# Gated cross-attention block, 16 x 256 tokens over 1601 keys: maxima split on VectorE and moved within SBUF, keys in four blocks, a beginning of its own for step 0, a new order of TensorE's work

## The reference

```python
def attention(v, k, q, ...):            # v = k = ctx, q = layernorm(x)
    qh, kh, vh = (split_heads(a @ w.T + b) for ...)
    logits = einsum('bhqd,bhkd->bhqk', qh, kh) / sqrt(8)
    out = einsum('bhqk,bhkd->bhqd', softmax(logits), vh)
    return out.reshape(B, S, 128) @ dense_w.T + dense_b

x = x + tanh(g_xattn[0]) * attention(ctx, ctx, layernorm(x))
# feed-forward: sigmoid gate of 8 experts, the two best, weights normalised, plus one shared expert
h = gelu(einsum('bsd,edh->bseh', xn, W1) + b1)
y = einsum('bseh,ehd->bsed', h, W2) + b2
x = x + tanh(g_ffn[0]) * (einsum('bse,bsed->bsd', gate_full, y) + gelu(xn @ Ws1 + bs1) @ Ws2 + bs2)
```

## Time and profile before

| | |
|---|---|
| median of 3 runs | 1435.47 us (1433.91 to 1437.52) |
| the profiled execution's own time | 1436.73 us |
| its span | 1434.9 us |
| TensorE matmul busy | 1241.7 us, 87% |
| VectorE busy | 1049.3 us, 73% |
| ScalarE busy | 1055.6 us, 74% |
| GpSimd busy | 418.7 us, 29% |
| granted TensorE clock, mean | 0.902 |

### The profile page before, as it was taken

The page is one execution under the profiler, slowest core; times in us unless marked ns, Lnnn a source line. Parts: engine busy times, 40 slices in busy tenths (PEclk is TensorE's granted clock), DMA queues, the critical chain, the costliest instruction groups (busy, mean ns, idle before and its releaser), DMA issues.

```text
span 1434.9 us, 29778 instructions
## 1 busy us (share of the span) xinstructions
PE 1241.7 (87%) x11555; PEld 458.9 (32%) x11555; DVE 1049.3 (73%) x1208; ACT 1055.6 (74%) x1962; POOL 418.7 (29%) x309
## 2 busy tenths in 40 slices
PE   2448889798989999899989999799979999799855
PEld 1112323232323433243323333243323433243224
DVE  8477778587768888688868878688768868689001
ACT  1008879587978799688968789688968889689741
POOL 7242224051333215151424125051423205010111
PEclk6568999798988999899989999899989999899786
DMA  7673634636273653737273744637173744501101
GB/s 213 114 149 69 150 70 98 140 84 129 53 164 70 139 119 87 147 81 149 52 169 61 170 87 99 139 82 146 47 167 67 165 92 96 102 11 33 31 14 45
DMA packets 71390, 147.13 MB, mean 103 GB/s; under 512 B 13705, under 2 KB 37970, under 8 KB 71250
## 3 DMA queue, kind: packets, MB, share of 16 engines
q1 hardware_dynamic: 71250, 145.24, 47.4%
HBM read 88.30 MB, written 56.91 MB: 101 GB/s over the span
## 4 chain that ended last, share of the span: by engine, by line
PE 66%; DMA 14%; ACT 5%; DVE 4%; SPq 4%; POOL 3%; issue 2%; POOLq 0%; ACTq 0%; DVEq 0%
PE o_ps L775 26%; PE a_ps L757 15%; PE b_ps L741 11%; DMA m_dram<-nm_parts 10%; PE a_ps L688 4%; PE a_ps L692 4%; ACT probs L573 3%; PE b_ps L720 2%; DVE run_max L901 2%; SPq L406 2%; DMA q_op<-m_dram 1%; SPq L397 1%; PE a_ps L684 1%; PE b_ps L723 1%; DMA q_op<-q_dram 1%
## 5 line engine op out<-in xcount | busy, mean ns | idle before, releaser
L901 DVE TENSOR_REDUCE run_max<-b_ps 128x2 f32<-128x1024 f32 x768 | 899.4, 1218 | 249.4 <-PE b_ps L741 246.0
L573 ACT ACTIVATE probs<-a_ps 128x512 f32<-128x512 f32 (+1 forms) x1664 | 901.9, 594 | 144.3 <-PE a_ps L757 127.4
L775 PE MATMUL o_ps<-probs,v_op 128*32 128x256 f32 (+3 forms) x4928 | 505.8, 483 | 2.3 <-ACT probs L573 1.2
L757 PE MATMUL a_ps<-q_op,k_op 51*128 51x256 bf16 (+1 forms) x3328 | 338.1, 283 | 46.4 <-DMA q_op<-m_dram 25.6
L741 PE MATMUL b_ps<-k_op,q_op 48*128 48x512 bf16 (+1 forms) x2048 | 325.6, 350 | 37.5 <-DVE run_max L901 24.2
L757 PEld LDWEIGHTS a_ps<-q_op,k_op 51*128 51x128 bf16 (+1 forms) x3328 | 112.9, 97 | 373.5 <-ACT probs L573 307.3
L741 PEld LDWEIGHTS b_ps<-k_op,q_op 48*128 48x128 bf16 x2048 | 88.7, 96 | 208.2 <-DVE run_max L901 95.9
L775 PEld LDWEIGHTS o_ps<-probs,v_op 128*32 128x32 f32 (+1 forms) x4928 | 98.4, 109 | 176.4 <-issue 93.8
L509 POOL TENSOR_TENSOR attn<-num,den_all 128x256 f32<-128x256 f32 x16 | 11.6, 728 | 440.3 <-DMA den_all<-r_dram 440.3
L688 PE MATMUL a_ps<-kctx,wk_s 128*128 128x400 f32 (+1 forms) x128 | 81.4, 734 | 55.7 <-DMA kctx<-ctx_t 49.9
L469 POOL TENSOR_TENSOR nm_parts<-nm_t,one 8x256 bf16<-8x256 f32 x32 | 19.3, 602 | 360.5 <-ACT nm_t L605 360.5
(11 more groups left out here) (100 smaller groups left out, 680.4 us busy)
## 6 DMA issues: line engine op xcount, KB each, us to landing
k_op<-k_dram SPq DMA_DIRECT2D x64, 600.4 KB, 9.5
k_dram<-k_parts SPq DMA_DIRECT2D x32, 600.4 KB, 6.0
kctx<-ctx_t SPq DMA_DIRECT2D x16, 800.5 KB, 12.5
vctx<-ctx_t SPq DMA_DIRECT2D x16, 800.5 KB, 11.8
k_dram<-k_parts SPq DMA_DIRECT2D x32, 400.2 KB, 7.0
o_dram<-o_s SPq DMA_DIRECT2D x32, 256.0 KB, 2.1
g_all<-g_dram SPq DMA_DIRECT2D x16, 512.0 KB, 6.4
k_dram<-k_parts SPq DMA_DIRECT2D x32, 200.1 KB, 6.7
```

The lines of the kernel that those rows point to most:

```text
L573: act.activation(probs[0:keys, unit % PB, :], a_ps[at % AB][0:keys, :], ACT.Exp, scale=SCALE).then_inc(a_taken, 1)
L757: last = pe.matmul(a_ps[(at + side) % AB][0:KEYS[t], SEQ * a:SEQ * a + SEQ], k_op[buf][rows, slot, 128 * t:128 * t + KEYS[t]], q_op[buf][r ...
L775: last = pe.matmul(o_ps[32 * j:32 * j + 32, cols], v_op[s // 2 % 2][0:KEYS[t], t, GP * (s % 2) + j, :], probs[0:KEYS[t], unit % PB, cols], ...
L901: dve.tensor_reduce(run_max[:, t, :, p, c:c + 1].rearrange("q v o -> q (v o)"), slot[:, :, :], AX.X, ALU.max).then_inc(b_taken, 1)
```

## The change

- The negated maxima are split into three bf16 parts on VectorE, right after `neg_max`, with queries on partitions (four operations of 128 x 16). T is a bf16 matmul against a bf16 identity and yields 24 rows; ScalarE copies them to `nm_t` (bf16), and six DMAs take them straight to `q_op`. `m_dram` and GpSimd's `split_maxima` are gone.
- GpSimd splits keys in four blocks, each after its own K unit; `divide` stands before the last block.
- Four part rows of the keys are stored where six were, in four DMAs for six; the operand rows are loaded as rows 0 to 3 and again rows 0 and 1, so an operand load has six DMAs for four. In both scratch tensors the halves of a head stand side by side. Queries are stored in six DMAs for twelve.
- SyncE's loop: `load_context("V")` moves to even steps, `load_context("K")` to behind `move_maxima`.
- The beginning: step 0's operands before other loads, ScalarE issues the first query stores, all tokens but the first 512 come later, and `first_maxima` puts all 26 maxima of step 0 and its T before everything except K units 1.0 to 1.3.
- `PLAN` has other strings.

```diff
-KPART = [0, 1, 2, 0, 1, 0]
-QPART = [0, 0, 0, 1, 1, 2]
+KPART = [0, 1, 2, 0, 0, 1]
+QPART = [0, 0, 0, 1, 2, 1]
+KEPT = 4
-PLACES = [(0, 3), (3, 5), (5, 6)]
+PLACES = [(0, 4), (4, 6)]
+Q_STORED = [(0, 3), (3, 5), (5, 6)]
...
-OP_DMAS = 4
+OP_DMAS = 2 * (len(PLACES) + 1)
+MAX_DMAS = 6
+DIVIDE_AT = [3, 3]
...
 PLAN = (
-    "SkSPVVPSkSPSkSPVVPSVPSVPSVPSVPSVPSVPSVPVSPyPSVVSPcSPVVPSSTkSPVVPSVPSVPSVPSVPdSPVVPVVPS",
...
+    "PSVPVSPSkVPSVPSVPSVPSkSPVVPSkSPVVPSVPSVPSVPVSPSkSPVVSPSvPSVVPSTVVPSdPvSPVVPSvPSVVPSVPVv",
...
 )
...
+def first_maxima():
+
+    scores = [event for event in ORDER[-2] if event[0] == "S"]
+    rest = [event for event in ORDER[-2] if event[0] != "S"]
+    first = [event for event in ORDER[-1] if event[0] == "S" and event[1] < SUNITS]
+    turn = [("A", ("T", 0, 0))]
+    return scores[:5] + rest + scores[5:], first + turn + [e for e in ORDER[-1] if e not in first + turn]
...
-        k_dram = nc.dram_tensor("k_dram", [2, 2, len(KPART), 64, CTX], BF16, kind="Internal").ap()
-        m_dram = nc.dram_tensor("m_dram", [2, 3, 2 * GP, SEQ], BF16, kind="Internal").ap()
+        k_dram = nc.dram_tensor("k_dram", [2, KEPT, 64, 2, CTX], BF16, kind="Internal").ap()
...
                 for side in range(2):
-                    sp.dma_start(k_op[buf][rows, :, :].rearrange("r (a p) c -> r a p c", a=2),
-                                 kd[:, :, pairs, :]).then_inc(op_in[buf], 16)
+                    for r0, r1 in PLACES:
+                        to = slice(SIDE * side + DH * r0, SIDE * side + DH * r1)
+                        sp.dma_start(k_op[buf][to, :, :], kd[0:DH * (r1 - r0), pairs]
+                                     .rearrange("r p a c -> r (p a) c")).then_inc(op_in[buf], 16)
...
             def move_maxima(s):
 
-                h = s % 2
-                sp.wait_ge(m_chain, 4 * (s + 1))
-                if s >= 2:
-                    sp.wait_ge(m_in[h], 32 * (s // 2))
-                sp.dma_start(m_dram[h].rearrange("n h q -> h n q"), nm_parts[:, :, :]).then_inc(m_written, 16)
-                sp.wait_ge(m_written, 16 * (s + 1))
+                sp.wait_ge(a_taken, a_done("T", s))
                 for side in range(2):
-                    sp.dma_start(q_op[s % 4][SIDE * side + ROWS:SIDE * side + MROWS, :, :],
-                                 m_dram[h, :, GP * side:GP * side + GP, :]).then_inc(m_in[h], 16)
+                    for n in range(3):
+                        row, col = SIDE * side + ROWS + n, 3 * GP * side + GP * n
+                        sp.dma_start(q_op[s % 4][row:row + 1, :, :], nm_t[col:col + GP, :]).then_inc(m_in[s % 2], 16)
...
+            store_keys(0)
+            load_operands(0)
+            load_context("K", kctx, 1, kctx_in)
+            load_tokens(1, 2, x_in[1])
+            load_operands(1)
             load(vctx, ctx_t[0]).then_inc(vctx_in, 16)
-            store_keys(0)
-            load_context("K", kctx, 1, kctx_in)
-            store_queries(0)
-            load_operands(0)
+            load_tokens(2, CHUNKS, x_in[2])
...
+                if s % 2 == 0 and 0 < b + 1 < BATCH:
+                    load_context("V", vctx, b + 1, vctx_in)
                 if s % 2 == 0 and 0 <= b - 1 < BATCH:
                     spread_sums(b - 1)
...
-                if s % 2 == 1 and b + 3 < BATCH:
-                    load_context("K", kctx, b + 3, kctx_in)
-                if s % 2 == 1 and 0 <= b + 2 < BATCH:
-                    load_context("V", vctx, b + 2, vctx_in)
                 if 0 <= s + 1 < STEPS:
                     move_maxima(s + 1)
+                if s % 2 == 1 and 0 < b + 3 < BATCH:
+                    load_context("K", kctx, b + 3, kctx_in)
...
-            def split_keys(b):
-
-                pool.wait_ge(a_taken, a_done("K", b, 3))
-                pool.wait_ge(k_written, 16 * PART_STORES * b)
-                split3(k_chain, 4 * (b - 1), k_t[:, :], [k_parts[:, i, :] for i in range(3)])
+            def split_keys(b, i):
+
+                pool.wait_ge(a_taken, a_done("K", b, i))
+                if i == 0:
+                    pool.wait_ge(k_written, 16 * PART_STORES * b)
+                cols = slice(KRUN[i][0], KRUN[i][0] + KRUN[i][1])
+                split3(k_chain, 4 * (len(KRUN) * (b - 1) + i), k_t[:, cols], [k_parts[:, n, cols] for n in range(3)])
...
                     for t in range(QTILES):
-                        last = pe.transpose(bank[0:2 * GP, 128 * t:128 * t + 128], neg_max[:, t, :], ident[:, :])
+                        last = pe.matmul(bank[0:6 * GP, 128 * t:128 * t + 128],
+                                         nm_parts[:, t].rearrange("q v n p -> q (v n p)"), ident_b[:, :],
+                                         start=True, stop=True)
...
-                                      ALU.max, negate=True).then_inc(nm_ready, 1)
+                                      ALU.max, negate=True).then_inc(nm_seq, 1)
...
+                    dve.wait_ge(nm_seq, 4 * s + 1)
+                    dve.tensor_copy(parts[0], whole).then_inc(nm_seq, 1)
+                    dve.wait_ge(nm_seq, 4 * s + 2)
+                    dve.tensor_tensor(whole, whole, parts[0], ALU.subtract).then_inc(nm_seq, 1)
+                    dve.wait_ge(nm_seq, 4 * s + 3)
+                    dve.tensor_copy(parts[1], whole).then_inc(nm_seq, 1)
+                    dve.wait_ge(nm_seq, 4 * s + 4)
+                    dve.tensor_tensor(parts[2], whole, parts[1], ALU.subtract).then_inc(nm_ready, 1)
```

More of the change, by code:

```diff
@@ L274, in flamingo_block @@
         op_in = [sem(f"op_in{i}") for i in range(4)]
-        m_written, m_in = sem("m_written"), [sem(f"m_in{i}") for i in range(2)]
+        nm_seq, m_in = sem("nm_seq"), [sem(f"m_in{i}") for i in range(2)]
         xn_seq = {w: sem(f"xn_seq_{w}") for w in norms}
@@ L314, in _ @@
                 load(dst, src).then_inc(const_in, 16)
-            for c in range(1, CHUNKS):
-                sp.dma_start(x_s[:, 4 * c:4 * c + 4, :], x[:, 4 * c:4 * c + 4, :]).then_inc(x_in, 16)
             def load_operands(s):
@@ L528, in split_queries @@
                 split3(q_chain, 4 * c, q_t[:, :], [q_parts[:, i, :] for i in range(3)])
-            def split_maxima(s):
-                pool.wait_ge(a_taken, a_done("T", s))
-                if s > 0:
-                    pool.wait_ge(m_written, 16 * s)
-                split3(m_chain, 4 * s, nm_t[:, :], [nm_parts[:, i, :] for i in range(3)])
             pool.wait_ge(ones_set, 2)
```

98 lines of the change are left out of this document (55 added, 43 removed).

## The result

The changed kernel takes **1313.31 us** (median of 4 runs, 1311.02 to 1322.63) against 1436.14 of the kernel before beside it (1433.91 to 1437.52). The ratio is 0.9158, 95% interval 0.9112 to 0.9205.

A forecast was written before the change was run, and what follows sets the result against it. TensorE was taken to bound the kernel, stopped by DMA waits that also lower its clock. 103 + 7 x 148.5 + 198 = 1340.5 us of span, plus 1.8 beside it: 1342 us, range 1316 to 1392.

The forecast's parts named there:

- The gaps close, the clock stays up: Phase 3 into phase 0: `kctx` and maxima waits close, so TensorE's clock stays up; gain in the steps 81 us.
- The first chain: Maxima from T to the next step's first P: 4.6 us of copy, issues and hop fit under TensorE's 8.1 us.
- if TensorE never waited: Steps: TensorE's work in four steps without waits or low clock, taken as 143.6 us.
- so I take 4.5: Steps: TensorE's small waits for ScalarE and VectorE grow from 2.5 to 4.5 us per four steps, from less slack.
- 145 (no residue): Low end of the four-step period, forecast at 148.5 us; the other end was 154.5.
- Keeps its chain; only the 5 us of low clock at its start go: From step 28's first P to the end: 203.3 us become 198.
- 8 us credited: Beginning: the new load and work order brings the first P from 110.8 to 102 us; ends 0 and 16.
- Rival D: Maxima late: subtractions wait for GpSimd, or small transfers stand behind operand loads; 28 times 1.5 us, 1384 us; chance 0.08.
- A (too even): Steps: gaps close but TensorE meets ScalarE or VectorE often; 4.5 us more per four steps, 1373 us; chance 0.16.
- B: Phase 3 boundaries: `kctx`, still last in the queue, lands as late as before; 63 us come back, 1405 us; chance 0.06.
- C: Both odd boundaries: K units wait for `kctx` behind the maxima, 14 times, 137 us; 1479 us, slower; chance 0.04.
- Covered, but thinly: Even steps: `den_all` comes some 4 us later, at about 25 us; the dense unit wants it at 28.

The follow-up runs named there:

- e10: Kernel before with keys split in four blocks and SyncE's new queue order; 1445.38 us, ratio 1.0086.
- e12: e10 plus the new layout of keys and queries in HBM; 1392.38 us, ratio 0.9685.
- e13: e10 plus the maxima split on VectorE and moved within SBUF by six DMAs; 1382.22 us, ratio 0.9595.
- e14: Kernel before with only the new way of the maxima (VectorE split, moved within SBUF); 1412.88 us, ratio 0.9818.
- e19: Changed kernel with twelve more 128x128 f32 copies on VectorE in each step; 1352.77 us, ratio 0.9418.
- e16: Changed kernel with both the old PLAN strings and the old beginning; 1323.28 us, ratio 0.922.
- e1: Kernel before with only the new PLAN strings, the list of TensorE's work; 1464.48 us, ratio 1.0203.
- e6: Changed kernel with the old beginning; 1311.28 us, ratio 0.9135.
- e2: Changed kernel with the old PLAN strings; 1336.84 us, ratio 0.9307.
- e22: e2 with GpSimd's two memsets of operand buffers held until VectorE has split the first keys; 1329.47 us, ratio 0.9268.
- e8: Changed kernel with the V context's load ahead of the operand loads in even steps; 1321.05 us, ratio 0.9172.
- e5: Changed kernel with the maxima stored to HBM in one DMA and read back in six; 1317.27 us, ratio 0.9178.

## Why the prediction was wrong in its size

The span came out 30 us short of the sum: 4 at the beginning (98.9 for 103), 17 in the steps and 9 at the end.

**The gaps close, the clock stays up: right.** No `kctx` wait after 110 us, no wait of a first P for the maxima in the steps, a clock of 1.00 from 110 to 1140 us for the 0.98 or more asked for, TensorE busy 97% of the steps. The first chain, for TensorE: T stands 8.4 us before the next P (8.1) and SyncE's six issues fit in it, though they take 3.79 us and not 1.7 (0.57 each, 192 of them, where a read from HBM took 0.27 at the median). That is 2.1 of the 3.5 us of room. The context lands in 4.7 us for 6.5. What was not said is that no part does this alone; e10, e12, e13 and e14 show it.

**The period: 148.5 predicted, 146.0 measured, 17 of the 29 us.** The sum was 143.6 for TensorE's work "if TensorE never waited", 0.2 of own work, "so I take 4.5" for small waits, and 0.2 of rounding up. Over the seven periods TensorE was busy 142.0 us and idle 4.0 on average. The work term, read in one full period, is right for a full one (143.66 in the row at 389.75), but it was used seven times, and the first two periods are lighter: 137.1 and 138.6 us. That is 1.8 of the 2.5 us. The idle term was 0.5 too large, although `vctx` (7.4 / 7 = 1.1 a period), which had no term, is in the 4.0. The waits for the other engines, which were to grow from 2.5 to 4.5 a period, did not: 17.0 us in the 28 steps, 2.4 a period, against 19.5 before. The last 0.5 of the idle time are pieces under 0.15 us. The argument that less slack brings more small waits is right in kind, as e19 shows, but 11 of 16.3 us more work for VectorE were covered there. The low end of "145 (no residue)" was nearer than the middle.

**The end: 198 predicted, 189.2 measured, 9 us.** The step that failed is "Keeps its chain; only the 5 us of low clock at its start go". It missed a second low stretch in step 31 of the kernel before (us, busy PE and PEld, DVE, ACT, POOL, granted clock, DMA share, GB/s):

```profile
1324.00:1334.00 10.00, 9.30 (x78) 3.06 (x76) 2.85 (x5) 9.34 (x17) 0.73 (x1) 1.00 0.47 107
1334.00:1344.00 10.00, 7.27 (x45) 1.25 (x44) 0.00 (x0) 7.43 (x13) 7.00 (x5) 0.70 0.01 2
1344.00:1354.00 10.00, 8.57 (x52) 2.27 (x52) 0.48 (x1) 5.91 (x11) 0.00 (x0) 0.50 0.08 29
```

and in the changed kernel, as far behind the first P of step 28:

```profile
1220.00:1230.00 10.00, 8.09 (x100) 2.19 (x92) 0.35 (x1) 9.73 (x19) 3.55 (x1) 1.00 0.01 2
1230.00:1240.00 10.00, 7.32 (x80) 1.86 (x80) 0.00 (x0) 9.29 (x19) 0.00 (x0) 1.00 0.10 34
1240.00:1250.00 10.00, 8.55 (x104) 2.31 (x102) 0.00 (x0) 9.76 (x19) 0.00 (x0) 1.00 0.01 2
```

3 + 5 us of full-clock work were missing in the second and third row of the kernel before. It is the list that avoids this, and not the DMAs: e16, with the DMAs in time and the old list, has it still and a rest of 203.2 us, as long as before:

```profile
1219.00:1229.00 10.00, 7.27 (x46) 1.32 (x44) 0.00 (x0) 7.16 (x12) 4.51 (x1) 0.65 0.01 1
1229.00:1239.00 10.00, 8.57 (x52) 2.20 (x48) 0.48 (x1) 6.45 (x13) 0.00 (x0) 0.50 0.08 29
```

and e1, the kernel before with the new list alone, has a clock of 1.00 from 1278 to 1408 us and a rest of 193.7. Even the 5 us at the start of the end did not go with the gap in front of step 28: e16 has no gap there and a clock of 0.66 from 1119 to 1129 us, the changed kernel 1.00. Which letters of the list do this (those of the feed-forward units in step 31, for one) is not shown.

**The beginning: 8 us credited, 12 measured, for the wrong reason.** The first S came at 45.9 us (44 predicted), T at 81.5 (82.4), the V units and QT took 6.3 us (8), the first P came at 98.9 (102). Each step of the working fits. But the credit was given to the new beginning, and e6 and e16 have their first P at 94.6 and 97.5 us without it. What moved the first P is the layout, 112.6 us in e10 and 101.6 in e12, and by 4 us the new way of the maxima (108.2 in e13). At the start of the kernel before, SyncE issues for 9.3 and 8.1 us, 6 key and 12 query stores; in e12 it is 4.8 us for four and 4.8 for six. That the credit comes near the measured 12 us is luck.

**VectorE's splitting: right.** 0.2 us each and 131 us of VectorE in four steps were taken; a full period has 130.5 to 130.7. The tile's subtraction, minimum/median/maximum in ns:

```profile
L935 DVE TENSOR_TENSOR neg_max<-neg_max,nm_parts x32: 174/176/853, 80.8 to 1213.8; 128x16 f32<-128x16 f32 x32
```

In e14, where GpSimd still splits 1601 columns at a time, the median is 175 ns and the longest 643. Rival D is out in the changed kernel: no first P of a step waits for `nm_t`. Its second form, small transfers behind large ones, came in e14 (10.3 us). Of its first form little is seen here: the lock that the Trainium skill describes on the page SBUF — State Buffer, section Who interferes with whom, seldom meets these operations, by the medians; that this is because GpSimd has little to do when T is due is argued. The lock met another operation, where I did not look for it: e2's copy of 10.5 us. The same section of the Trainium skill names casts, copies and `tensor_scalar` as operations that can take the port pair shared with GpSimd, and says that two-input `tensor_tensor` meets only GpSimd's reads. The traces agree on both. In the changed kernel the same `TENSOR_TENSOR` of 128x400 took 1.29 us beside GpSimd's split of the queries, which reads, and 0.58 beside a memset, which only writes; a `CAST` beside the memset took 7.89 us in e22 and 10.50 in e2. The rows of VectorE and those of GpSimd beside them:

```profile
16.32 1.29 DVE L952 TENSOR_TENSOR k_parts<-k_t,k_parts 128x400 bf16<-128x400 f32 x1
16.10 1.09 POOL L488 TENSOR_TENSOR q_parts<-q_t,one 128x512 bf16<-128x512 f32 x1 [3.45 <-ACT q_t L624]
21.13 11.17 POOL L556 MEMSET k_op<- 128x6404 bf16 x2
21.45 0.58 DVE L952 TENSOR_TENSOR k_parts<-k_t,k_parts 128x400 bf16<-128x400 f32 x1
```

The six small transfers did not pay 2.0 us each one after another either. The section of the Trainium skill that the prediction took this figure from is on DMAs that GpSimd issues, and SyncE issued these; here no first P waited for them, though SyncE is through with the six only 3.4 us before it.

**Rivals.** A (too even) at 4.5 us more did not come; 5.3 us came only with 16.3 us of extra load. B and C needed a landing of 9 us or more for `kctx`; in the steps it was 4.2 to 5.8 from 165 us on. B's mechanism is real all the same: e13, with six stores, has landings of up to 9.8 us and waits of 26.3 us, and it is the layout that keeps it away. "Covered, but thinly" of the dense unit was right: e8, which delays it a little, paid 15.1 us there. The cover that broke was the one of `vctx`, of which I had only said where its load went: 10.3 to 18.5 us from issue to landing, behind 1.4 MB in the even step.

## What to carry to other kernels

When several DMAs in one queue feed one point of an in-order engine, the gap goes only when the last of them is in time: parts of it alone read as harm (e1), as nothing (e10) or as 2% (e14), and all together as 8%. Undo parts from the full change and add them to the old kernel, since the two sides tell different things: the new way of the maxima takes the ratio from 1.009 to 0.960 on top of e10, and giving its second hop back to the full change costs nothing that can be told (e5).

Cost the clock's low stretches one by one over the whole span, ahead of and behind the steps too. Terms that you "keep" deserve the same windows as those that you change.
